# A decoder on one core: the merged order of two sequences' stages, and where each engine's loop begins, written anew

## The reference, cut to what matters

```
for each of 16 sequences x (128 x 256):
    h = layernorm(x);  q, k, v = h Wq, h Wk, h Wv; rotate q, k          # 32 heads, windowed attention
    x += softmax([scores in a window of 32 | sink]) v  Wo
    h = layernorm(x);  16 heads of 16 against the 128 rows of the context;  x += (...) o_w
    h = layernorm(x);  router over 64 experts, top 8: x += h*sum(w) + w @ expert_bias
    h = layernorm(x);  32 heads of 8 (as two halves of 16) and a memory term;  x += mix of both
    h = layernorm(x);  scores of h and context, summed over the sequences
then, over all sequences: a retention-like mix, a router over 8 experts, the experts' products, the sums
```

## Time and profile before

| what | value |
|---|---|
| median of 3 runs (lowest to highest) | 2018.16 us (2017.08 to 2021.89) |
| the profiled execution: its own time | 2016.88 us |
| span of its trace | 2015.1 us |
| busy share of the span: PE, DVE, ACT, POOL | 69%, 67%, 32%, 10% |
| start of `l0` of sequence 0 in turn 3, 4 (DVE) | 643.57, 837.98 us |

### The profile page before, as it was taken

One profiled execution on the slowest core, in us unless ns is written; L12 is line 12 of the kernel. 1 busy time (PEld: TensorE's weight loads), 2 busy tenths in 40 slices (PEclk: granted clock), 3 DMA queues, 4 the chain that ended last, 5 costly groups with the idle time before them and its releaser, 6 DMA issues.

```text
span 2015.1 us, 37567 instructions
## 1 busy us (share of the span) xinstructions
PE 1388.9 (69%) x14598; PEld 1065.2 (53%) x14598; DVE 1346.3 (67%) x2684; ACT 640.3 (32%) x1482; POOL 207.5 (10%) x401
## 2 busy tenths in 40 slices
PE   1775777568757876786678677867775555569990
PEld 1664565456545655564556455645664444436660
DVE  3877786768676867786677777777867566633332
ACT  2233423332342234323523252334223422223330
POOL 0010001000100000000000000100010036410006
PEclk9786778678767865786688568857785576679995
DMA  9800000000000000000000000000000023111114
GB/s 349 269 1 1 1 13 1 1 2 12 1 1 13 1 1 1 13 2 0 1 13 1 1 1 13 1 1 1 2 1 0 34 95 133 52 61 58 59 50 126
DMA packets 47742, 70.10 MB, mean 35 GB/s; under 512 B 4737, under 2 KB 42049, under 8 KB 46017
## 3 DMA queue, kind: packets, MB, share of 16 engines
q1 hardware_dynamic: 44480, 59.08, 8.7%
q0 software_dynamic: 3072, 8.39, 1.2%
HBM read 36.40 MB, written 31.06 MB: 33 GB/s over the span
## 4 chain that ended last, share of the span: by engine, by line
issue 66%; PE 16%; DVE 9%; POOL 6%; ACT 2%; SPq 1%; DMA 0%; POOLq 0%; DVEq 0%; ACTq 0%
PE ps L859 11%; POOL rstd L1270 2%; PE ps L863 2%; POOL experts L763 1%; SPq L814 1%; POOL rstd L1269 1%; DVE experts L635 1%; PE ps L451 1%; PE ps L961 1%; ACT big L1194 1%; PE ps L378 1%; PE ps L424 0%; DVE ptf L1436 0%; DVE st L1510 0%; ACT experts L491 0%
## 5 line engine op out<-in xcount | busy, mean ns | idle before, releaser
L1194 ACT ACTIVATE big<-ps,st 128x128 f32<-128x128 f32 x768 | 206.1, 405 | 176.7 <-DVE st L1512 176.7
L961 PE MATMUL ps<-ident,big 128*128 128x128 f32 x1024 | 193.9, 355 | 83.6 <-ACT big L1194 63.3
L961 PEld LDWEIGHTS ps<-ident,big 128*128 128x128 f32 x1024 | 161.7, 186 | 107.2 <-ACT big L1194 77.7
L1200 ACT ACTIVATE ptf<-ps 128x1024 f16<-128x1024 f32 x128 | 131.9, 1041 | 105.4 <-PE ps L961 104.2
L1436 DVE TENSOR_TENSOR ptf<-ps,ptf 128x1024 f16<-128x1024 f32 x128 | 152.6, 1219 | 17.5 <-ACT ptf L1200 17.4
L1510 DVE TENSOR_REDUCE st<-ps 128x8 f32<-128x1024 f32 x96 | 117.0, 1219 | 69.8 <-PE ps L859 69.8
L1269 POOL TENSOR_TENSOR rstd<-mv,eps 128x1 f32<-128x1 f32 x80 | 15.2, 189 | 1409.5 <-DVE mv L1327 1409.5
L859 PE MATMUL ps<-wo,qhl 128*128 128x256 f32 x512 | 145.6, 451 | 0.0
L859 PEld LDWEIGHTS ps<-wo,qhl 128*128 128x128 f32 x512 | 116.1, 232 | 22.6 <-issue 0.6
L863 PE MATMUL ps<-k_h,qhl 32*128 32x64 f16 x2048 | 82.3, 227 | 48.8 <-issue 33.8
L859 PE MATMUL ps<-experts,ptf 128*128 x468 | 109.7, 385 | 0.0
(11 more groups left out here) (316 smaller groups left out, 3445.8 us busy)
## 6 DMA issues: line engine op xcount, KB each, us to landing
scratch<-mixT SPq DMA_DIRECT2D x10, 1920.0 KB, 16.7
big<-in_gu SPq DMA_DIRECT2D x8, 1024.0 KB, 5.0
ptf<-scratch SPq DMA_DIRECT2D x39, 128.0 KB, 2.0
scratch<-ptf SPq DMA_DIRECT2D x39, 128.0 KB, 1.7
kf<-in_dn SPq DMA_DIRECT2D x8, 512.0 KB, 5.9
xin<-in_x SPq DMA_DIRECT2D x16, 128.0 KB, 2.2
cin<-in_ctx SPq DMA_DIRECT2D x16, 128.0 KB, 3.4
big<-in_wq SPq DMA_DIRECT2D x2, 1024.0 KB, 6.4
```

Of the source, the lines that this page charges most:

```text
L961: m = pe.transpose(ps_f(u, j // 4, P, (j % 4) * P), big[u][:, j * P:(j + 1) * P], ident[:])
L1194: m = f(big[u][:, c], ps_all[u][:, c], ACT.Exp, scale=scale, bias=st32[u][:, 3, j:j + 1])
L1200: f(pt_h[u][:, c], ps_all[u][:, c], ACT.Copy).then_inc(sig(f"pt{n}h{h}", u), 1)
```

## The change

All four strings keep the same items (each stage of both sequences once). POOL's is unchanged. In the other three, two things are new.

**Where the string begins.** PE's loop began at `1:a31` and begins at `0:a33`; ACT's began at `0:a0s` and begins at `0:a15s`; DVE's began at `0:l0` and begins at `0:a7q`. The items between the old and the new beginning carry a plus now, for sequence 0 too, so `all_turns` sets both turns to 0 before the stretch ahead. Written out from the first to the last item, turning a string this way changes nothing in the order: the stretch before the loop gets longer and the one behind it shorter. Only the place of the branch moves.

**The merge.** Each sequence's own order on each engine is as before. What differs is which stage of one sequence stands before which of the other. From `l0` of sequence 0 to `1:a12` the differences are few: ACT does `1:e01` before `0:v0h` and not behind it; PE does `0:a21` before `1:T00` and not behind `1:T01`; DVE does `1:l00 1:l01` before `0:k0l` and not behind it. From `1:a12` to the following turn's `1+ql1` nearly all of the merge is new: sequence 1 goes further ahead of sequence 0 (for instance `1:a15v` before `0:a8`; `1:a17v 1:n3 1:xT3` before `0:l10`; `1:a22b` before `0:l3a0`; `1+l0 1+n0 1+a0v` before `0:s3b0`; and at the end `0:a31v 0:a32v` behind `1+ql1`).

```diff
-    turn[1] = 0
+    turn[:] = [0, 0]
```

```diff
 TENSOR_TURN = """
-1:a31 1:a32 0:a0 1:a33 0:a1a 0:a1b 0:a1c 0:a20 1:T00 1:T01 0:a21 0:a22 0:a23 1:a50 1:a51 1:a52 1:a53 0:a3m
-0:a30 0:a31 0:a32 0:a33 1:a60 1:a61 0:T00 0:T01 1:tr1 1:a7 0:a50 0:a51 0:a52 0:a53 1:pk1 0:a60 1:c10 1:c11
-0:a61 1:T10 1:T11 0:tr1 0:a7 1:pv1 1:atr 1:prj 0:pk1 1:tr2 0:c10 0:c11 1:a15 0:T10 1:a16 0:T11 1:a17 0:pv1
-0:atr 1:tr3 0:prj 1:a19 0:tr2 0:a15 1:pk3 0:a16 0:a17 1:memp 1:c3a0 1:c3a1 0:tr3 0:a19 1:T3a0 1:T3a1 1:pv3a
-0:pk3 1:c3b0 1:c3b1 0:memp 1:T3b0 0:c3a0 1:T3b1 0:c3a1 1:pv3b 0:T3a0 0:T3a1 1:tr4 1:mx1 0:pv3a 1:mx2 0:c3b0
-0:c3b1 0:T3b0 1+a0 0:T3b1 1+a1a 1+a1b 0:pv3b 1+a1c 1+a20 1+a21 0:tr4 1+a22 1+a23 0:mx1 1+a3m 0:mx2 1+a30
+0:a33 1:a60 1:a61 0:T00 0:T01 1:tr1 1:a7 0:a50 0:a51 0:a52 0:a53 1:pk1 0:a60 1:c10 1:c11 0:a61 1:T10 1:T11
+0:tr1 0:a7 1:pv1 1:atr 1:prj 1:tr2 0:pk1 1:a15 0:c10 0:c11 1:a16 1:a17 0:T10 0:T11 1:tr3 1:a19 0:pv1 0:atr
+0:prj 1:pk3 0:tr2 0:a15 1:memp 1:c3a0 1:c3a1 0:a16 0:a17 1:T3a0 1:T3a1 0:tr3 0:a19 1:pv3a 1:c3b0 1:c3b1 1:T3b0
+0:pk3 1:T3b1 0:memp 0:c3a0 0:c3a1 1:pv3b 0:T3a0 1:tr4 0:T3a1 1:mx1 1:mx2 0:pv3a 1+a0 0:c3b0 0:c3b1 1+a1a 1+a1b
+0:T3b0 0:T3b1 1+a1c 1+a20 0:pv3b 1+a21 1+a22 0:tr4 1+a23 0:mx1 0:mx2 1+a3m 1+a30 1+a31 1+a32 0+a0 1+a33 0+a1a
+0+a1b 0+a1c 0+a20 0+a21 1+T00 1+T01 0+a22 0+a23 1+a50 1+a51 1+a52 1+a53 0+a3m 0+a30 0+a31 0+a32
 """
 SCALAR_TURN = """
-0:a0s 1:e00 0:v0h 1:e01 0:k0h 1:h00 1:h01 0:qh0 0:qh1 1:o0a 0:e00 0:e01 0:h00 0:h01 1:rq 1:rk 0:o0a 1:qT1
-1:e10 1:e11 1:h10 1:h11 0:rq 0:rk 0:qT1 0:e10 1:a15s 0:e11 0:h10 0:h11 1:a19s 0:a15s 1:qT3 1:e3a0 1:e3a1
-1:h3a0 1:h3a1 0:a19s 0:qT3 1:e3b0 1:e3b1 1:h3b0 1:h3b1 0:e3a0 0:e3a1 0:h3a0 0:h3a1 1:a31s 0:e3b0 0:e3b1 1+a0s
-0:h3b0 0:h3b1 1+v0h 1+k0h 0:a31s 1+qh0 1+qh1
+0:a15s 1:e3a0 1:e3a1 1:h3a0 1:h3a1 0:a19s 1:e3b0 1:e3b1 1:h3b0 0:qT3 1:h3b1 0:e3a0 0:e3a1 0:h3a0 0:h3a1 1:a31s
+1+a0s 0:e3b0 0:e3b1 0:h3b0 0:h3b1 1+v0h 1+k0h 0:a31s 1+qh0 1+qh1 0+a0s 1+e00 1+e01 0+v0h 1+h00 1+h01 0+k0h
+0+qh0 0+qh1 1+o0a 0+e00 0+e01 0+h00 0+h01 1+rq 1+rk 0+o0a 1+qT1 1+e10 1+e11 1+h10 1+h11 0+rq 0+rk 0+qT1 1+a15s
+0+e10 0+e11 0+h10 0+h11 1+a19s 1+qT3
 """
...
 VECTOR_TURN = """
-0:l0 0:n0 1:s00 0:a0v 1:s01 0:k0 1:n00 1:n01 0:v0 0:k0l 1:l00 1:l01 0:q1 0:q2 0:q3 0:q4 0:ql0 0:ql1 1:o0b
-0:s00 0:s01 0:n00 0:n01 1:a6v 1:n1 1:xT1 0:l00 0:l01 1:a7v 1:a7q 1:a7k 0:o0b 1:a8 1:s10 1:s11 0:a6v 0:n1 0:xT1
-1:l10 1:l11 0:a7v 1:a11 1:a12 0:a7q 0:a7k 1:a13 1:n2 0:a8 1:xT2 0:s10 1:a15v 0:s11 1:a15t 1:a16v 0:l10 0:l11
-1:a17v 0:a11 1:n3 0:a12 1:xT3 0:a13 1:a19v 0:n2 0:xT2 1:a19e 0:a15v 0:a15t 0:a16v 1:pk3v 0:a17v 1:mv 0:n3
-1:s3a0 0:xT3 1:s3a1 0:a19v 1:l3a0 1:l3a1 0:a19e 1:a22a 1:s3b0 0:pk3v 1:s3b1 0:mv 0:s3a0 1:l3b0 1:l3b1 0:s3a1
-1:a22b 1:n4 0:l3a0 1:xT4 0:l3a1 1:a31v 0:a22a 1:a32v 0:s3b0 1+l0 0:s3b1 1+n0 1+a0v 0:l3b0 0:l3b1 1+k0 0:a22b
-1+v0 0:n4 1+k0l 1+q1 0:xT4 1+q2 0:a31v 1+q3 1+q4 1+ql0 0:a32v 1+ql1
+0:a7q 1:a13 0:a7k 1:n2 1:xT2 1:a15v 0:a8 1:a15t 0:s10 1:a16v 0:s11 1:a17v 1:n3 1:xT3 0:l10 0:l11 1:a19v 0:a11
+0:a12 1:a19e 0:a13 0:n2 1:pk3v 0:xT2 0:a15v 1:mv 0:a15t 1:s3a0 0:a16v 1:s3a1 0:a17v 0:n3 0:xT3 1:l3a0 1:l3a1
+0:a19v 1:a22a 1:s3b0 1:s3b1 0:a19e 1:l3b0 0:pk3v 0:mv 1:l3b1 0:s3a0 0:s3a1 1:a22b 1:n4 1:xT4 0:l3a0 0:l3a1
+1:a31v 1:a32v 1+l0 0:a22a 1+n0 1+a0v 0:s3b0 0:s3b1 0:l3b0 0:l3b1 1+k0 1+v0 0:a22b 1+k0l 0:n4 1+q1 0:xT4 1+q2
+1+q3 1+q4 1+ql0 1+ql1 0:a31v 0:a32v 0+l0 0+n0 1+s00 0+a0v 1+s01 0+k0 1+n00 1+n01 0+v0 1+l00 1+l01 0+k0l 0+q1
+0+q2 0+q3 0+q4 0+ql0 0+ql1 1+o0b 0+s00 0+s01 0+n00 0+n01 1+a6v 1+n1 1+xT1 0+l00 0+l01 1+a7v 1+a7q 1+a7k 0+o0b
+1+a8 1+s10 1+s11 0+a6v 0+n1 0+xT1 1+l10 1+l11 0+a7v 1+a11 1+a12
 """
```

## The result

The changed kernel is slower, by about half of what was forecast: 2028.2 us median of 7 runs (2022.69 to 2035.43) against 2018.16 (2017.08 to 2021.89), a ratio of 1.0047 with a 95% interval of 1.0029 to 1.0065. That is +10 us; the forecast was +22. The profiled execution took 2025.26 us.

A forecast was written before the change was run, and what follows sets the result against it. No engine is full; the in-order merge, through DVE's pauses for late inputs, sets the turn. Terms sum to +3.8 us in six turns and -0.3 in two, +22 together: 2040 us, forecast's range 2025 to 2062.

The forecast's parts named there:

- swaps in the first part: First part of the turn: DVE's pauses before `1:n01` and `0:q2` go, 3.3 us gained a turn (bounds 1.0 to 4.6).
- new merge: From `1:a12` to the end of `1+ql1`: DVE's pauses grow, costing 3.0 us a turn (3 gained to 5 lost).
- old beginning goes: From `1+ql1` to `1:a6v`: removing the old branch pauses gains 2.1 us in each of six turns.
- PE's new beginning: Before `0:a33`: PE's first branch pause stays, the second may return, 4.2 us in six turns (3.1 to 5.6).
- DVE's new beginning: Before `0:a7q`: DVE's branch pause reaches `1:a15v` with 2.0 us in six turns (1.2 to 2.7).
- The sign and its mechanism: Slower, chance 0.60: moving the loops' beginnings can hide a branch pause but not remove it; likeliest time 2040 us.
- the walk of the new merge: DVE's new order stepped from `1:a12` on: pauses from 30.3 to 35.3 us, 3.0 a turn without the branch's 2.0.
- The walk's checkpoints: Forecast stage times on DVE, old to new: `1:a15v` 735.0 to 736.6, `0:l3b0` 814.2 to 821.2, end 836.1 to 841.1.
- Faster by overlap: Rival, chance 0.22: from `1:a12` to `1+ql1`, sequence 1's lead fills pauses, shrinking them by 5 us a turn: 1976 us.
- Faster by PE's clock: Rival, chance 0.08: PE's clock held high behind `1:a12` gives 4.4 us a turn, 35 in all: 2005 us.
- No change: Rival, chance 0.10: the branches at the loops' beginnings cancel and the merge is neutral: about 2016 us.
- The turn of 198 us: Sign expected in the changed trace: a turn takes 198 us; under 194.5 us the prediction would be wrong.

The follow-up runs named there:

- the wider extra work: The kernel before plus one unused DVE maximum of about 2.3 us ahead of `1:a13` in every turn: 2019.75 us, ratio 1.001.
- the narrower: The kernel before plus one unused DVE maximum of about 1.2 us ahead of `1:a13` in every turn: 2021.32 us, ratio 1.0006.

## Why the prediction came out half wrong

The terms of the sum, each with the kernel that measured it:

| term | predicted, us in all | measured |
|---|---|---|
| swaps in the first part, -3.3 x 8 | -26.4 | -15.3 (2002.9), alone |
| new merge, +3.0 x 8 | +24.0 | +26.9 with branches hidden; with the old beginnings +15.4 on top of the swaps, +4.4 without them |
| both together | -2.4 | 0 (2018.26) |
| old beginning goes, -2.1 x 6 | -12.6 | -20.4 on the new merge; -31.9 on the old one with the swaps |
| PE's new beginning, +4.2 x 6 | +25.2 | +18.5 |
| DVE's new beginning, +2.0 x 6 | +12.0 | +11.2 |
| sum | +22.2 | +10 |

**The sign and its mechanism were right.** The branch at a loop's beginning moves with it, a bare pause is paid, and the two old ones were cheaper together than the two new ones. The places of the pauses, their number (six) and the missing pause at L1337 came as said; `1:n01` starts right behind `1:n00`.

**The steps that failed are two terms of the beginnings**, "the old beginning goes" at 2.1 us and "PE's new beginning" at 4.2: their mechanism held, their sizes did not. The first was read from a turn with and one without a branch, up to `1:a6v`. On the new merge the old pair costs 20.4 / 6 = 3.4 us, on the old merge with the swaps 31.9 / 6 = 5.3. The granted clock is nearly the same in the two stretches of that reading (0.77 and 0.76). What differs is other pauses: the turn without a branch waits 1.74 us before `1:n01` and 1.71 before `0:q2`, turn 4, which has one, only 1.36 and 0.22:

```profile
856.24 1.22 DVE L1427 TENSOR_REDUCE st<-big 128x16 f32<-128x1024 f32 x1 [1.36 <-ACT big L1190]
...
865.69 1.23 DVE L1389 TENSOR_TENSOR ptf<-ps,sinI 128x1024 f32<-128x1024 f32 x1 [0.22 <-PE ps L863]
```

So the 2.1 is what is left after those pauses, and the swaps that remove them stand in a term of their own. The two hang together: they were put at -26.4 - 12.6 = -39.0 us and are -47.2 (2018.2 to 1971.0, swaps made and both branches hidden). No run hides the branches without the swaps, so how the 47.2 divides on the old merge rests on the order in which the two are taken. The second failed term left room for half of PE's second pause, with no row to size it by; that pause does not return at `0:a33`, and the term is 18.5 / 6 = 3.1, about the one pause.

The two make (20.4 - 12.6) + (25.2 - 18.5) = 14.5 us, a little more than the 12 by which the sum was off; the rest goes the other way, since swaps and merge cancel rather than gain 2.4. That they cancel as forecast is in part luck: with the old beginnings the swaps give 15.3 us and not 26.4, and the merge on top of them costs 15.4 and not 24.0. Taken in another order, each step a kernel that ran, it is the same picture: swaps and hidden branches -47.2 us (-39.0 predicted), the new merge +26.9 (+24.0), the new beginnings +30.3 (+37.2).

**What was right of the parts.** DVE's new beginning (2.0 predicted, 1.9 measured) and the walk of the new merge (3.0 predicted, 3.4 with the branches out of the way). The walk's checkpoints came 0.6 to 3.0 us earlier than walked: set to the same `1:a12` (1.57 us later here), `1:a15v` starts at 736.0 (736.6 walked), `1+a0v` at 810.8 (813.7), `0:l3b0` at 820.0 (821.2) and `0:l0` at 840.2 (841.1). The pause before `0:l3b0` is 5.58 us and not 3.9, because the stages ahead of it ran still earlier than its end. The swaps give 1.9 a turn on the old merge instead of 3.3, measured with the old branches in place, beside which the pauses that the swaps remove are shorter (1.36 and 0.22 us above).

**The rivals.** Faster by overlap needed the merge to cost less than 0.2 us a turn; it costs 1.9 to 3.4 with the swaps (0.5 without them, still more than 0.2). Faster by PE's clock: the clock of the second part is 0.67 against 0.66, no change. No change was the nearest: merge and swaps are neutral, but the beginnings are not. The turn of 198 us is not seen in the changed kernel (196.24); it is in three of six turns when PE alone stays at its old place (197.98).

The Trainium skill (Runtime: NRT & Kernel Launch, "Instruction fetch mechanics") says that a taken branch outside of what is loaded makes the engine wait for the target's code. The runs agree and add that the wait is free inside another one: with both branches in waits of 2.9 us and more no such pause is left, and 30.3 us are gained on the new merge, 31.9 on the old one (2002.9 to 1971.0).

**What stays open.** Why PE's second pause comes behind `1:a31` (1.9 to 2.7 us in all kernels that begin there) and not behind `0:a33`. And whether the clock is what makes sums of terms come out short in the changed kernel as well: it is shown for the wider extra work, not the case for the narrower, and only argued for the rest, from turns that repeat. Why PE at its old place and DVE at its new one cost 8 us more together than the sum of each alone is open too.

## What to carry to other kernels

Put each loop's beginning where its engine waits longest for another engine anyway; here that gave 30 to 32 us, twice the best change of the order, and moving beginnings elsewhere only moved the pauses. If branches cannot be hidden, let the engines' pauses fall at the same time: here two that overlap cost about as much as one (20.4 us), and two far apart cost both or more (30.3 to 38.3). Price a pause by taking it away in a kernel of its own, not by comparing two turns.

## What the runs showed that was not expected

- Turns take a few lengths again and again, 3.4 to 3.5 us apart: 187.7 us (old merge with swaps and hidden branches), 191.1 (new merge, hidden), 194.5 (before; the new merge with old beginnings, with the swaps and without; on it most turns with PE at either place alone or DVE at `0:l0` alone; both kernels with extra work), 198.0 (old merge with new beginnings; the last turns with PE old and DVE new). PE's two bare pauses of 3.39 and 2.00 us and a single one of 3.0 to 3.7 both lead from 191.1 to 194.5. But other kernels lie between: the changed kernel alternates (196.8 and 195.8), the swaps alone take 191.1 to 194.2, DVE at `0:a7q` alone 192.3 to 196.3, PE new with DVE old 195.0 to 198.2, and the new merge with hidden branches and `1+k0` earlier 189.0 to 191.0. Why lengths recur is not shown.
- 2.28 us of extra DVE work a turn on the path cost nothing per turn, because waits on the way took up a part and PE's full clock, some 3 us earlier, the rest.
- DVE's pause for a branch is 2.54 to 2.83 us behind a copy of 0.42 us in the changed kernel, 1.8 to 2.1 behind a 1.23 us instruction on the old merge, and 3.0 to 3.3 at the same stage on the new one, where it follows an instruction of 0.41 us (the last of `0:a32v`).
